# Units of two convolutions issued two by two on TensorE, a second pair of PSUM banks for the transposed v, and a rearranged opening

## The reference

```python
xn = srms(x)
u = silu(xn @ u_w.T + u_b)
v = silu(xn @ v_w.T + v_b)
# a long convolution of v along the rows' axis, and one along the columns' axis, each channel with its own
# 127 coefficients; these come from two small networks (rpe1, rpe2) of the position
out = tno(v, -3, ...rpe2...) + tno(v, -2, ...rpe1...)
out = u * out
return out @ o_w.T + o_b + x
```

## Time and profile before

| | us |
|---|---|
| median of 3 runs (772.76 to 774.32) | 772.85 |
| the profiled execution | 775.57 |
| its span | 773.8 |
| TensorE busy (matmul) | 746.2, 96% |
| ACT / DVE / POOL busy | 532.8 / 483.2 / 280.6 |
| DMA queue q1, share of 16 engines | 73.9% |
| mean granted TensorE clock | 0.989 |

### The profile page before, as it was taken

The page is one execution under the profiler, slowest core; times in us unless marked ns, Lnnn a source line. Parts: engine busy times, 40 slices in busy tenths (PEclk is TensorE's granted clock), DMA queues, the critical chain, the costliest instruction groups (busy, mean ns, idle before and its releaser), DMA issues.

```text
span 773.8 us, 19177 instructions
## 1 busy us (share of the span) xinstructions
PE 746.2 (96%) x7202; PEld 679.4 (88%) x7202; DVE 483.2 (62%) x860; ACT 532.8 (69%) x864; POOL 280.6 (36%) x188
## 2 busy tenths in 40 slices
PE   8699999989999999899999999998999999999998
PEld 7699999979999998799999999997999999887875
DVE  6577755347788889444444444445445554688877
ACT  3466678856667666777777777774667666677665
POOL 2433333111211122645555554520000000498985
PEclk9899999999999999999999999998999999999999
DMA  9645565489888986488888888859555555699996
GB/s 210 176 147 174 170 169 172 177 223 192 180 184 189 198 189 196 134 274 270 271 271 269 268 267 269 274 173 215 132 129 130 133 138 130 194 286 323 328 302 204
DMA packets 132308, 161.15 MB, mean 208 GB/s; under 512 B 69772, under 2 KB 97420, under 8 KB 132236
## 3 DMA queue, kind: packets, MB, share of 16 engines
q1 hardware_dynamic: 131948, 160.15, 73.9%
q10 hardware_dynamic: 288, 0.00, 0.0%
HBM read 109.49 MB, written 50.63 MB: 207 GB/s over the span
## 4 chain that ended last, share of the span: by engine, by line
PE 79%; DMA 9%; DVE 6%; SPq 2%; POOL 2%; issue 1%; ACT 1%; DVEq 0%; POOLq 0%; ACTq 0%
PE ps L1045 22%; PE ps L1152 16%; PE ps L1124 10%; PE ps L1137 10%; PE ps L1068 7%; PE ps L1058 7%; PE ps L1034 3%; DMA u_in<-u_dram 3%; DMA x_e<-in_x_eT 2%; DMA free_rows<-in_x 2%; PE ps L1071 1%; POOL u_in L537 1%; DMA u_dram<-u_out 1%; DVE x_e L953 1%; DVE n_tmp L715 1%
## 5 line engine op out<-in xcount | busy, mean ns | idle before, releaser
L537 POOL TENSOR_TENSOR u_in<-u_in,v 128x1152 f32<-128x1152 f32 (+2 forms) x67 | 174.9, 2619 | 150.6 <-DMA u_in<-u_dram 140.4
L894 DVE COPY toepB<-stage 64x512 f32<-64x512 f32 x144 | 107.2, 745 | 81.8 <-PE ps L1152 73.2
L944 DVE TENSOR_TENSOR g<-ps,g 128x512 fp32r<-128x512 f32 (+1 forms) x192 | 125.3, 679 | 43.7 <-ACT g L610 39.8
L1152 PE MATMUL ps<-toepB,vt 128*128 128x128 f32 x1152 | 142.3, 277 | 1.8 <-POOL toepB L521 1.8
L1152 PEld LDWEIGHTS ps<-toepB,vt 128*128 128x128 f32 x1152 | 136.7, 194 | 2.2 <-POOL toepB L521 2.0
L1045 PE MATMUL ps<-wu,xh 97*128 97x288 f32 x512 | 121.1, 302 | 0.0
L1045 PE MATMUL ps<-wv,xh 97*128 97x288 f32 x512 | 119.3, 309 | 1.3 <-DVE xl L802 1.0
L802 DVE TENSOR_TENSOR xl<-ps,xh 96x512 fp32r<-96x512 f32 x64 | 43.6, 682 | 108.0 <-ACT xh L582 107.9
L1058 PE MATMUL ps<-ident,u_in 128*128 128x128 f32 (+1 forms) x768 | 100.2, 273 | 3.8 <-POOL u_in L537 2.4
L1068 PE MATMUL ps<-g,wo 128*96 128x512 f32 x384 | 101.9, 400 | 0.0
L638 ACT COPY vt<-ps 128x1024 f32<-128x1024 f32 x72 | 73.0, 1013 | 38.7 <-PE ps L1124 38.7
(11 more groups left out here) (83 smaller groups left out, 1037.8 us busy)
## 6 DMA issues: line engine op xcount, KB each, us to landing
stage<-a_dram SPq DMA_DIRECT2D x144, 256.0 KB, 4.3
u_in<-u_dram SPq DMA_DIRECT2D x64, 576.0 KB, 5.4
u_dram<-u_out SPq DMA_DIRECT2D x48, 576.0 KB, 3.3
x_e<-in_x_eT SPq DMA_DIRECT2D x64, 192.0 KB, 4.3
out<-x_e SPq DMA_DIRECT2D x64, 192.0 KB, 4.1
u_dram<-u_in SPq DMA_DIRECT2D x16, 576.0 KB, 3.1
x_n<-in_x SPq DMA_DIRECT2D x16, 384.0 KB, 5.6
xa<-in_x SPq DMA_DIRECT2D x64, 96.0 KB, 4.6
```

Of the source, the lines that this page charges most:

```text
L537: return nc.gpsimd.tensor_tensor(out=tile, in0=tile, in1=v[:, start // 2:end // 2, bass.ds(t * NB, NB)].rearrange("p c n e -> p n c e"), o ...
L894: nc.vector.tensor_copy(toepB[n % 2][rows, :, rows], stage[half][n % STAGES][rows, axis].rearrange("p k c -> p c k")[:, :, ::-1]).then_inc ...
L944: nc.vector.tensor_tensor(out=low, in0=ps[0:w, bank], in1=high.bitcast(f32), op=ALU.subtract).then_inc(gl_ready, 1)
L1152: last = nc.tensor.matmul(ps[:, SET_BANK[n % 2] + c // NB, (c % NB) * P:(c % NB + 1) * P], vt[n % 2][:, c], toepB[n % 2][:, c], start=Fals ...
```

## The change

- Phase C on TensorE goes by pairs of units: columns of n and n+1, rows of n and n+1, then the transposes of v of n+2 and n+3. The transposed v of odd units has banks 6-7. ACT goes by pairs too (vt, vt, y, y). The last two units' crossed parts are copied by DVE.
- `toepB[1]` of half 0 moves to bytes that only the x_e tiles and the raw output weights use, so it waits for `wo_split` and no longer for the stored u. In half 1 it stays on `u_out`.
- Half 1: the first two stage loads are issued one by one in the last two steps of B0; the last x addition on DVE stands ahead of the first Toeplitz copy; the transposes of unit 1 wait for it (`o_ready`). The x_e loads wait for the last rows, not the last columns.
- Opening: squares of the first chunk's steps 2 and 3 and of chunk 1 move to ACT; chunk 1's norms follow on DVE at once instead of after two steps; 22 warming transposes in place of 34.
- Start of B0: `transpose_x`, `high_x`, `low_x` of step 1 stand early in step 0.

```diff
-        toepB = [place(f"toepB{k}", [P, UNIT, P], V + (32768, 28672)[k]) for k in range(2)]
+        toepB0, toepB1, toepB2 = (place(f"toepB{k}", [P, UNIT, P], V + (32768, 18432, 28672)[k]) for k in range(3))
+        toepB = ((toepB0, toepB1), (toepB0, toepB2))
+        x_sq1 = place("x_sq1", [P, CH * NB, E], V)
-        WARM = (12, 34, 8)
+        WARM = (12, 22, 8)
...
@@ sync
-                sp.wait_ge(columns_done, TILES * (UNITS * half + UNITS))
+                sp.wait_ge(conv_done, UNITS * half + UNITS)
...
+                        if t >= STEPS - 2:
+
+                            sp.wait_ge(y_transposed, NCH * t)
+                            load_stage(1, t - (STEPS - 2))
                         if not first or r >= 2:
                             sp.wait_ge(o_stored[0][r % 2], 32 * c + 16 * (r // 2))
                             load_xe(0, t, r)
                         if not (first and r == 0):
                             store_out(0, t - 1, r + 1)
                         if t == STEPS - 1:
-
-                            sp.wait_ge(y_transposed, NCH * t)
-                            for n in range(2):
-                                load_stage(1, n)
                             sp.wait_ge(y_transposed, NCH * (t + 1))
                             load_stage(1, 2)
@@ gpsimd
-            for r in range(FIRST, CH):
-                scale_a0(r, 0, r)
-                for k in range(2 * (r - FIRST), 2 * (r - FIRST) + 2):
-                    square_a0(1, k)
...
-            pool.wait_ge(ua_stored[1], 16 * (STEPS // 2))
-            zero(toepB[1], 2)
+            pool.wait_ge(wo_split, 6)
+            zero(toepB[0][1], 2)
@@ scalar
+            def squares_of(source, target, chunk):
+                act.wait_ge(x_all_loaded, 32 * (chunk + 1))
+                nc.scalar.activation(target, source, ACT.Square).then_inc(opening_squared, 1)
+
+            late = slice(NB * FIRST, NB * CH)
+            squares_of(x_chunk(0)[:, late], x_sq[:, late], 0)
             act.wait_ge(weights_loaded, 4 * 16)
...
+            squares_of(x_chunk(1), x_sq1[:], 1)
             high_x(0, 0)
...
-                evacuate_vt(0)
-                for n in range(UNITS):
-                    if n:
-                        evacuate_y(n - 1)
-                    if n + 1 < UNITS:
-                        evacuate_vt(n + 1)
-                    elif half == 0:
-                        high_x(STEPS, 0)
-                evacuate_y(UNITS - 1)
+                for n in range(0, UNITS, 2):
+                    for k in range(2):
+                        evacuate_vt(n + k)
+                    for k in range(2):
+                        if half == 0 and n + k == UNITS - 2:
+                            high_x(STEPS, 0)
+                        evacuate_y(n + k)
@@ vector
+            dve.wait_ge(opening_squared, 1)
+            sum_opening(FIRST, CH - FIRST, x_sq[:, NB * FIRST:NB * CH])
+            opening = norms(FIRST, CH - FIRST, 1, 0)
+            run(opening[:6])
             low_x(0, 0)
-            opening = norms(FIRST, CH - FIRST, 1, 0)
-            run(opening[:9])
+            run(opening[6:])
+
+
+            dve.wait_ge(opening_squared, 2)
+            sum_opening(CH, CH, x_sq1[:])
             low_x(1, 1)
-            run(opening[9:])
...
-                toeplitz(0, 0)
                 if half:
                     add_x(0, STEPS - 1, STEPS - 1, 16 * (STEPS // 2))
+                toeplitz(0, 0)
...
-                    dve.wait_ge(ua_stored[1], 16 * (STEPS // 2))
+                    dve.wait_ge(wo_split, 6)
...
-                        run(itertools.islice(pieces, 4))
+                        run(itertools.islice(pieces, 5))
@@ tensor
-                    wait(pe, vt_ready, N)
+                    wait(pe, vt_ready, N - 1)
...
                 transpose_v(0)
-                for n in range(UNITS):
-                    if n < 2:
-                        pe.wait_ge(silu_done, PAIRS * STEPS * (half + 1) - 1 + n)
-                    along_columns(n)
-                    if n + 1 < UNITS:
-                        transpose_v(n + 1)
-                    elif half == 0:
+
+                if half:
+                    pe.wait_ge(o_ready, STEPS)
+                else:
+                    pe.wait_ge(a_ready, 2)
+                transpose_v(1)
+                for n in range(0, UNITS, 2):
+                    for k in range(2):
+                        if n == 0:
+                            pe.wait_ge(silu_done, PAIRS * STEPS * (half + 1) - 1 + k)
+                        along_columns(n + k)
+                    along_rows(n)
+                    if half == 0 and n + 2 == UNITS:
+                        pe.wait_ge(vt_ready, UNITS)
                         transpose_x(STEPS, 0)
-                    along_rows(n)
+                    along_rows(n + 1)
+                    if n + 2 < UNITS:
+                        for k in range(2):
+                            transpose_v(n + 2 + k)
```

More of the change, by code:

```diff
@@ L244, in conv_through @@
         def conv_through(engine, half, unit):
-            before = half * (Y_PARTS * (UNITS - 1) + 1)
-            if unit < UNITS - 1:
+            before, last = half * (Y_PARTS * (UNITS - 2) + 2), unit - (UNITS - 2) + 1
+            if last <= 0:
                 engine.wait_ge(conv_out, before + Y_PARTS * (unit + 1))
             else:
-                engine.wait_ge(conv_out, before + Y_PARTS * unit + 1)
-                engine.wait_ge(conv_crossed, 2 * (half + 1))
+                engine.wait_ge(conv_out, before + Y_PARTS * (UNITS - 2) + last)
+                engine.wait_ge(conv_crossed, 4 * half + 2 * last)
         block = ctx.enter_context(nc.Block())
@@ L673, in body0 @@
                             silu_v(1, t, pair)
+                        high_x(STEPS + 1, 1)
                     for k in range(2):
@@ L681, in body0 @@
                         silu_u(1, t, pair, u_out, ub_stored, 16 * t)
-                    if start:
-                        high_x(STEPS + 1, 1)
             def body1(c, first, last):
@@ L840, in phase_a @@
                         low_x(CH * c + (r + 1), r + 1)
-                    if first and r == 1:
-                        sum_a0(1)
                     if r == 0 and not last:
                         pieces = norms_a0(c + 1, c if networks and not first else None)
-                    if r < 2 and not last and not first:
+                    if r < 2 and not last:
                         half_way = len(pieces) // 2
+                        if first:
+                            half_way = (len(pieces), 0)[r]
                         run(pieces[half_way * r:half_way * (r + 1)])
@@ L849, in phase_a @@
                         rpe_norm(c)
-                    if first and r == 2:
-                        run(pieces)
                     if networks and r == 3:
@@ L961, in body0 @@
                     banks = [Y_BANK + (NCH * r + k) % 2 for k in range(NCH)]
+                    if start:
+                        low_x(STEPS + 1, 1)
                     low_g(t, 0, banks[0], g)
@@ L966, in body0 @@
                     low_g(t, 2, banks[2], g)
-                    if start:
-                        low_x(STEPS + 1, 1)
             def body1(c, first, last):
```

67 lines of the change are left out of this document (34 added, 33 removed).

## The result

Four executions of the changed kernel, 749.46 to 755.12, have a median of **751.20 us**; four of the kernel before, 771.90 to 774.32, one of 772.81. The ratio is 0.9726, 95% interval 0.9684 to 0.9767: faster by 2.7%. The forecast, 748.2 by its sum, was 3.0 us too low, inside its range. Run again on another occasion, unchanged, the two gave 750.97 (six executions) and 772.91 (eight); so each has two profiles, and the spans can be cut at the same places of the program. All numbers of the table are us. A stretch ends at the first matmul of the place named, or at the end of the last one; the last column is after again less before again.

What follows compares the result with a forecast made beforehand. TensorE, its matmuls busy 96% of the span, was taken to bound the kernel. Terms -12.6 + 0.9 - 2.8 - 4.0 - 5.3 - 0.8 = -24.6 us took the profiled 775.57 to 751.0, for the median 748.2; range 742 to 757.

Steps and rivals of the forecast that it cites:

- Switches, -12.6 + 0.9: Middle of phase C: 36 pairs of array switches go, -12.6 us, a pair taking 7.67; +0.9 allowed for late Toeplitz tiles.
- (a): Phase C switches: only the named idle time goes, 6.4 us for 12.6, time 754; chance 0.13.
- (c): Phase C: the hand-over through ACT becomes the bound and the kernel gets slower, 800 us; chance 0.04.
- (d): Phase C: switches cost the same in pairs and DVE in half 0 gives back the rest, 760 us; chance 0.05.
- Starts of phase C, -2.8 and -4.0: Less TensorE waiting at phase C's two starts: -2.8 us in half 0, -4.0 us in half 1.
- 1.4 us late next: Start of phase C, half 0: columns of unit 1 would wait 1.4 us for their coefficients.
- (b): Phase C's starts and the opening stay late, over 2 us each with half clock behind, 756 us; chance 0.12.
- Opening, -5.3: Opening: the 5.92 us wait for chunk 1's norms goes, step 1 at 20.9, 36.4 for 42.22; -5.3 us taken.
- Start of B0, -0.8: Start of B0: step 1's 1.49 us wait for its low x goes, -0.8 us, between -1.5 and +1.
- The step that turned a sum into a median: Whole kernel: the profiled execution lay 2.7 us above the median, so 751.0 for the profile became 748.2 for the median.

Runs made afterwards that it cites:

- after again: The changed kernel run again unchanged and profiled a second time: 750.97 us, ratio 0.9720 against the kernel before.
- before again: The kernel before, run again unchanged and profiled a second time: 772.91 us, ratio 0.9997.
- four_switches: The changed kernel with TensorE's pair order made columns, rows, columns, rows, then both units' transposes: 759.29 us, ratio 0.9811.
- old_opening: The changed kernel with the opening of the kernel before (warming transposes, squares, sums, low parts): 756.77 us, ratio 0.9787.
- all_fixed: The changed kernel with four one-instruction moves together: GpSimd's chunk 2 square, VectorE's step 1 low part, SyncE's u store and x_e load: 753.42 us, ratio 0.9754.
- gate_waits: The changed kernel with GpSimd's first gate of B0 made to wait for the last norms: 751.64 us, ratio 0.9733.
- old_starts: The changed kernel with half 0's toepB of unit 1 back on u_out and half 1's first stage loads late again: 759.77 us, ratio 0.9810.
- square_later: The changed kernel with GpSimd's square of chunk 2, step 0, moved behind the scaling of step 3: 752.26 us, ratio 0.9735.
- b0_start_undone: The changed kernel with B0's step 1 x work back at step 0's end and gated u's first transposes waiting for the whole gate: 752.39 us, ratio 0.9735.
- pairs_alone: The kernel before with only phase C's pairs (TensorE's and ACT's order, second pair of banks): 765.30 us, ratio 0.9878.
- late_norms: The changed kernel with the last four norm pieces moved behind the hand-over of units 34 and 35: 753.77 us, ratio 0.9759.
- norms_in_step: The changed kernel with the last four norm pieces moved to the end of B0's step 0: 752.06 us, ratio 0.9731.

## Why the prediction was right, and where it was short

**Switches, -12.6 + 0.9: right.** The pair takes 7.67 as forecast, and 36 times 0.36 is 13.0. Undone alone it gave back 12.1 in the two C phases. Rivals (a), (c) and (d) fall: the named idle time fell from 12.9 to 6.1 us, about half of what went; ACT had a vt ready 0.9 us ahead of its rows, where 0.8 was counted; DVE gave nothing back in the middle. What the runs show is the price of the order; that the array's change of tile size is what costs it is the reading that fits, and no run tells it from another effect of the same places.

**Starts of phase C, -2.8 and -4.0: right as a sum.** Over the bare pace of 36 units (144.5 before, 138.0 after) half 0 lay 4.9 above and now 2.2, half 1 6.0 and now 2.8: -5.9 where -2.8 - 4.0 + 0.9 was written. Undone, they gave back 7.2. The 1.4 us late next in half 0 showed as 1.04. In half 1 the next was DVE's addition of x, 1.37 for the 0.4 written, and POOL's zeroes cost nothing. Rival (b) falls: the clock was 1.0 at both.

**Opening, -5.3: right in size**, -4.6 and -5.8 in the pairs of profiles, 3.2 to 4.3 where it alone was undone. Of its places, 20.9 for step 1 and 36.4 for step 5 were met (20.87; 36.58 and 37.62 in the two profiles); the transposes of step 4, said near 29, came at 30.16 and 32.19, the later one behind a stretch at half clock.

**Start of B0, -0.8: the step that failed.** The edit itself is worth that or more. But the term was worked out from the wait for step 1's low x, with the rest of the start left as it was. The wait of the first projection, 0.41 and 0.29 us in the two profiles of before, was taken to stay; it became 1.47 and 3.75. From the transposes of step 5 on, B0 took 183.3 to 183.9 us in all fourteen profiles, so its differences lie at its start:

| profiles | last Toeplitz copy on DVE, ahead of the rows' end | POOL's first gate, ahead of it | norm piece held there | wait of the first projection | B0 |
|---|---|---|---|---|---|
| before, before again | 6.7 | 4.7, 4.8 | yes | 0.41, 0.29 | 213.5, 213.4 |
| four_switches | 6.4 | 2.8 | no | none | 211.9 |
| after, old_opening | 4.2, 4.3 | 2.1, 1.6 | no | 1.47, 1.40 | 213.1, 213.1 |
| all_fixed, gate_waits | 3.8, 4.1 | 1.1, 1.8 | no | 1.84, 1.62 | 214.5, 217.2 |
| after_again, old_starts, square_later, b0_start_undone | 3.7 to 4.2 | 2.3 to 2.8 | yes | 3.67 to 4.09 | 216.4 to 218.2 |
| pairs_alone | 4.3 | 2.3 | yes | 2.62 | 217.3 |

The table shows what changed. With pairs on TensorE, DVE comes to its last Toeplitz copy 3.7 to 4.3 us ahead of the rows' end, with single units 6.4 to 6.7 us ahead (four_switches differs from the changed kernel in that order alone). All that DVE has behind this copy moves with it: the last norm pieces, the copy of a part of unit 34, the low part of x. A piece held 2.3 to 2.4 us beside the gate was covered by the rows before; now TensorE waits for it. The changed kernel also put the copy of 1.41 us ahead of the low part: pairs_alone, which hasn't got it there, waited 1.1 to 1.5 us less than the four others with the hold. No run takes that copy away in the changed kernel itself. In the five profiles with a piece held at the first gate and pairs, and in all_fixed and gate_waits, the clock fell behind the wait; in the first three rows of the table it stayed at 1.0. In late_norms and norms_in_step, where the pieces stood elsewhere, later gates held one, and B0 took 217.5 and 214.8. A term of +3 in place of -0.8 in one of two executions, as in the two profiles of the changed kernel, would have given about 750.

The step that turned a sum into a median was weak too. The profiled execution of before lay 2.7 above its median and that of after 1.7 below its own; 26.1 between them is 21.6 between medians. That the forecast for the profile (751.0) was above the profile (749.5), and for the median below the median, comes of that and of the scatter of B1; that the sum fitted the profile so well is in part luck, as that profile had no hold.

**Open:** whether the hold is what makes all the slower executions of the changed kernel slow. norms_in_step takes its cost away at the start and its median is still 752.1; only the profiled execution can be looked into. The ten executions of after lie by and large the higher the lower their mean clock (0.998: 749.3 to 749.8; 0.994 to 0.997: 750.8 to 753.9; 0.986: 755.1), and gate_waits shows half clock behind a wait of 1.62 where after had none behind 1.47. So the clock falls at this start for more than the hold. The length of one wait doesn't settle it either: in old_starts it stayed at 1.00 behind 3.11 us.

## What to carry to other kernels

Where blocks of quarter-array and full-array matmuls alternate, count the switches and batch the blocks two by two if banks allow: here 0.36 us for every two units in the middle of the phase. The starts keep it only if the two units' operands are there in time, and the end of the phase gave some of it back: 12.1 us in the two phases were 7 to 8 in the whole. When the order of a phase changes, look at how far ahead of its end the other engines now are: a hold that was covered before, and stood in the old trace already, can become a wait. A wait taken away in an opening that several engines share is worth what the next one leaves, and small moves there (four of them) gave nothing.

## What the runs showed of the hardware

A small DVE operation that starts beside a GpSimd tensor_tensor stands until that one ends: 2.43 beside 2.41, 2.64 beside 2.74, 2.62 to the end of two gates of together 3.12, where it takes 0.17 alone. It happened to SCALAR_TENSOR_TENSOR and TENSOR_SCALAR on n_tmp: in the fourteen profiles 428 of them started inside such an operation, and every one ended 0.02 to 0.10 us behind its end; all others took 0.15 to 0.19 us. The copies of coefficients out of `stage` were held as well (the toepA copy at 661.99 in before took 2.77 us for 0.64). MEMSET (0.48), RECIPROCAL (0.25) and the copies out of PSUM (1.41 us for two, with or without a gate beside them) kept their times. The Trainium skill, "SBUF — State Buffer", Who interferes with whom, states this as an exclusive lock on a port pair that the two engines share, which an operation of DVE with two SBUF inputs, or one in a two-port mode, must get for its whole length. The traces agree with it; a reader of that section, with the piece of 2.42 us in before's own trace, could have asked before the run what the hold would cost.
